# Cross attention on one core: inputs laid out by the host, the full-mask flag multiplied into Q, one key buffer, the loop written out

## The chip, the core and the metric

The kernel runs on one core of one Trainium2 chip. The core has TensorE (PE in the rows), VectorE (DVE), ScalarE (ACT), GpSimd (POOL) and SyncE (SP, which here only issues DMAs). Each works through its own instructions in order, and they meet at semaphores that the kernel sets and waits for by hand. The metric is the time of one execution on the device in microseconds. What the host does to the arrays before the launch isn't in it.

## The reference

```python
q = split_heads(x   @ W_Q.T)      # x: [4, 1024, 256], 16 heads of 16
k = split_heads(ctx @ W_K.T)      # ctx: [4, 77, 256]
v = split_heads(ctx @ W_V.T)
scores = q @ k.T / 4              # [4, 16, 1024, 77]
scores = where(mask == 1, -1e9, scores)
p = softmax(scores)
out = (p @ v).reshape(B, S, 256) @ W_O.T + x
out = (out - mean) * rsqrt(var + 1e-5) * gamma + beta     # over the 256
```

The mask is int32, [4, 1024, 77], and can mask all keys of a row. Such a row has equal scores, so its softmax is uniform.

## The kernel before, in words

The 4096 query rows are cut into 8 blocks of 512, two for each of the 4 batches. A block has 8 steps, one for each pair of heads, and its work is spread over three rounds of the loop, so that the engines work on several blocks at once.

Two blocks ahead (`n + 2`): x is scaled by a flag that is 0 for rows with all keys masked (`act_xs`, `pool_xs`), turned by TensorE (`pe_x_t`, steps 0 and 1, copied out by `act_x_t`), and projected to Q in two halves of 8 heads (`pe_q`, steps 2 and 3). Q is split into a high f16 part (`act_q_high`) and a low f16 part, the remainder (`dve_q_low`). SyncE writes both to a scratch tensor in DRAM (`store_q`) and reads them back by head (`load_q`) into `R`, which holds for each head the rows of a wide contraction: Q high, Q low, Q high again, the mask of the 77 keys (`load_mask`), and a row for the negated maximum. There are two buffers `R`, used in turn. The heads are loaded in the three groups of `GROUPS`: heads 0 to 5, 6 to 11, 12 to 15.

One block ahead (`n + 1`): the row maxima. `pe_max` computes scores with the queries on the partitions, in 12 units (3 groups by 4 tiles of 128 queries, 6 or 4 heads each, two banks in turn), `dve_max` reduces each to a maximum. `UNITS_AT` places two units in each of steps 0 to 5. `pe_nm` turns the maxima, `act_nm` copies them and ScalarE's queue issues the DMA that puts them in R's last row.

The block itself (`n`): `pe_scores` computes the transposed scores, keys on the partitions, less the maxima; ScalarE takes the exponential; `pe_pv` multiplies with the values, four heads side by side, after each 4 pairs; `dve_turn` turns the result and takes the reciprocal of the sum; `pool_norm` normalizes; `dve_ctx_e` turns back. The output projection of block `n - 1` (`pe_out`, f32, steps 6 and 7), the residual and the layer norm follow one and two rounds later.

The order on each queue is written out by hand in `body` of each engine. SyncE's matters here. In a round it stores half 0 of Q, then for each head group loads the mask, and Q (lines 316 to 325), and half 1's store stands between group 0's mask and group 0's Q:

```python
store_q(sp, n + 2, h, b + 1, 0)
for g in range(len(GROUPS)):
    sp.wait_ge(scores_done, PAIRS * n + GROUPS[g][1] // 2)
    load_mask(sp, n + 2, h, g)
    if g == 0:
        store_q(sp, n + 2, h, b + 1, 1)
```

The first and the last batch are written out; the two in the middle are one loop with a register. Because addresses in the loop depend on it, the keys and values of a batch are copied to fixed buffers (`kb_max`, `kb_scores`, `v_now`).

The setup turns the four weights, the context and the first blocks' x and masks on TensorE, projects K and V for all batches, and sends K through a DRAM scratch tensor like Q. Then it makes the whole of block 0's maxima (all 12 units of `pe_max` in a row).

Of the kernel before, what the change touches and what calls it, by code (L numbers as in the profile page):

```python
# [21 lines left out]
BLOCKS = BATCH * SEQ // BLOCK  # L45
TILES = BLOCK // P
HALVES = D // P
PAIRS = HEADS // 2
STEPS = PAIRS
QROWS = 3 * DK  # L50
MASK_ROW = QROWS
MAX_ROW = MASK_ROW + KEYS
KROWS = MAX_ROW + 1
BIG = 32768.0

GROUPS = [(0, 6), (6, 12), (12, 16)]
# [8 lines left out]
NM_AT = 5  # L65
XT_AT = (0, 1)
Q_AT = (2, 3)
OUT_AT = (6, 7)
STATS_AT = (0, 1, 2, 3)
VARIANCE_AT = 5  # L70
APPLY_AT = (6, 7)

CTX_AT = (1, 5)

LAST_VARIANCE_AT = 4
LAST_APPLY_AT = (5, 6)

POOL_TILES = TILES - 1

RLOADS = 3  # L80

GROUPS_OF = [[g for g, (lo, hi) in enumerate(GROUPS) if lo < (e + 1) * PAIRS and hi > e * PAIRS] for e in range(HALVES)]

MASK_PARTS = [(0, 1), (1, 2), (2, 4), (4, BLOCKS)]
MASK_LOADS = [(0, 1), (1, 4), (4, BLOCKS)]
MASK_TURNS = [(0, 1), (1, 2), (2, 4), (4, 6), (6, BLOCKS)]

WO_U, MASK_U = 5, 7
KSCALE = 1.0 / float(DK) ** 0.5

def cross_attention(nc, x, ctx_in, mask, w_q, w_k, w_v, w_o, gamma, beta, out):
    stack = ExitStack()
    with stack:
# [6 lines left out]
        def sem(name):  # L101
            return stack.enter_context(nc.semaphore(name))

        q_scratch = [nc.dram_tensor(f"q_scratch{i}", [HEADS, 2, DK, BLOCK], F16, kind="Internal").ap() for i in range(2)]
        k_scratch = nc.dram_tensor("k_scratch", [2, HEADS, DK, BATCH * KEYS], F16, kind="Internal").ap()

        x_all = sb("x_all", [P, BLOCKS * TILES, D])
        mask_all = sb("mask_all", [P, BLOCKS * TILES, KEYS], I32)  # L110
        w_t = [sb(f"w_t{i}", [P, HALVES, D]) for i in range(4)]
        ctx_sb = sb("ctx_sb", [KEYS, BATCH, D])
# [12 lines left out]
        minus_half = sb("minus_half", [P, TILES])
        all_masked = sb("all_masked", [P, BLOCKS * TILES])
        not_full = sb("not_full", [P, BLOCKS * TILES])
        not_full_big = sb("not_full_big", [P, BLOCKS * TILES])
        mask16 = sb("mask16", [P, BLOCKS * TILES, KEYS], F16)
        mask_t = sb("mask_t", [KEYS, BLOCKS, BLOCK], F16)  # L130
        xs = sb("xs", [P, TILES, D])
        x_t = sb("x_t", [P, HALVES, BLOCK])
        q16 = sb("q16", [P, HALVES, 2, BLOCK], F16)
        R = [sb(f"R{i}", [KROWS, HEADS, BLOCK], F16) for i in range(2)]
        neg_max = sb("neg_max", [P, TILES, HEADS], F16)
        neg_max_t = sb("neg_max_t", [HEADS, BLOCK], F16)
        probs = sb("probs", [P, PAIRS, 2, BLOCK])
        y = [sb(f"y{i}", [P, TILES, D]) for i in range(2)]

        spare = probs[:, 4:6, :, :].rearrange("p s i q -> p (s i q)").rearrange("p (i t d) -> p i t d", t=HALVES, d=D)  # L140
        w_in = [spare[:, i, :, :] for i in range(3)] + [y[1][:, 0:HALVES, :]]
        mask_eq = probs[:, 6:8, :, :].rearrange("p s i q -> p (s i q)").bitcast(F16)[:, 0:BLOCKS * TILES * KEYS].rearrange(
            "p (t k) -> p t k", k=KEYS)
        ctx_q = sb("ctx_q", [P, 2, BLOCK // 32, 32])
        rden = sb("rden", [P, 2, BLOCK // 32])
        ctx_n = sb("ctx_n", [P, HALVES, BLOCK // 32, 32])
        ctx_e = [sb(f"ctx_e{i}", [P, HALVES, BLOCK]) for i in range(2)]
        bn = sb("bn", [P, TILES, 6])
# [6 lines left out]

# [4 lines left out]
        work16 = work_ps[:, :].bitcast(F16)  # L160
        pv16 = pv_ps[:, :].bitcast(F16)
        max16 = [t[:, :].bitcast(F16) for t in max_ps]

        s_w = [sem(f"s_w{i}") for i in range(3)]
        s_ctx = sem("s_ctx")
        s_gb = sem("s_gb")
        s_x = [sem(f"s_x{i}") for i in range(BLOCKS)]
        s_mask = [sem(f"s_mask{i}") for i in range(len(MASK_LOADS))]
        s_ident = sem("s_ident")  # L170
        s_zero = sem("s_zero")
        w_t_done, w_t_ready = sem("w_t_done"), sem("w_t_ready")
        c_t_done, c_t_ready = sem("c_t_done"), sem("c_t_ready")
        k_done, k_high, k_low = sem("k_done"), sem("k_high"), sem("k_low")
        v_done, v_ready, v_ones = sem("v_done"), sem("v_ready"), sem("v_ones")
        s_k_out = sem("s_k_out")
        s_kb = sem("s_kb")
        tail_ready = sem("tail_ready")
        s_tail = [sem("s_tail_max"), sem("s_tail_scores")]
        kb_scores_ready, kb_max_ready, v_now_ready = sem("kb_scores_ready"), sem("kb_max_ready"), sem("v_now_ready")  # L180
        eq_ready, full_ready, not_full_ready, mask16_ready = sem("eq_ready"), sem("full_ready"), sem("not_full_ready"), sem("mask16_ready")
        xs_ready = sem("xs_ready")
        mask_t_done, mask_t_ready = sem("mask_t_done"), sem("mask_t_ready")
        x_t_done, x_t_ready = sem("x_t_done"), sem("x_t_ready")
        q_done, q_high, q_low = sem("q_done"), sem("q_high"), sem("q_low")
# [8 lines left out]
        bn_ready, mv_ready, ve_ready, rstd_ready, shift_ready = sem("bn_ready"), sem("mv_ready"), sem("ve_ready"), sem("rstd_ready"), sem("shift_ready")  # L194
        y_normed, y_gamma, y_beta = sem("y_normed"), sem("y_gamma"), sem("y_beta")
        y_dve = sem("y_dve")
        y_last = sem("y_last")
        s_y = [sem(f"s_y{i}") for i in range(2)]

        x_rows = x.rearrange("b (m p t) d -> p (b m) t d", p=P, t=TILES)
        mask_rows = mask.rearrange("b (m p t) k -> p (b m) t k", p=P, t=TILES)
# [13 lines left out]
        def store_q(sp, m, par, b, e):  # L216

            sp.wait_ge(q_low, HALVES * m + e + 1)
            if not isinstance(b, int) or b > 0:
                for g in GROUPS_OF[e]:  # L220
                    sp.wait_ge(s_R[par][g], 16 * RLOADS * b)
            for part in range(2):
                sp.dma_start(q_scratch[par][e * PAIRS:(e + 1) * PAIRS, part, :, :], q16[:, e, part, :]).then_inc(s_q_out[e], 16)  # L223

        def load_mask(sp, m, par, g):

            lo, hi = GROUPS[g]
# [786 lines left out]
```

## Time and profile before

| | |
|---|---|
| median of 3 runs | 223.49 us (222.67 to 225.48) |
| span of the profiled execution | 224.2 us |
| TensorE matmuls busy | 177.5 us (79%) |
| VectorE busy | 148.1 us (66%) |
| ScalarE busy | 113.7 us (51%) |
| GpSimd busy | 83.4 us (37%) |
| DMA | 33.35 MB, mean 149 GB/s |

The profile is one execution. Its record holds the span, 224.2 us, and that is its own time here; it lies between the slowest and the middle one of the three timed runs. Shares of the span mix the setup, the steady rounds and the tail, so a stage has to be read from the windows and from the instructions in order of time. In those, "[5.97 <-DMA R<-neg_max_t]" behind an instruction means that its engine stood idle for 5.97 us before it and what released it was a DMA that wrote R from neg_max_t.

### The profile page before, as it was taken

How to read it: one execution, taken by the hardware profiler on the slowest of the kernel's cores; microseconds unless marked ns; L12 is line 12 of the kernel's file. 1: busy time of each engine (PE TensorE's matmuls, PEld its weight loads, DVE VectorE, ACT ScalarE, POOL GpSimd, SP SyncE). 2: the span in 40 equal slices, each digit the busy share in tenths (PEclk: the TensorE clock that was granted, in tenths of full speed). 3: DMA queues.
4: the chain of work that ended last, by engine and by line, in shares of the span. 5: the costliest groups of instructions: out<-in, count | busy, mean ns of one | idle time of the engine just before them, and what ended most of it. 6: DMA issues, size and time to landing. Idle time of an engine off the chain costs nothing.

```text
span 224.2 us, 3953 instructions
## 1 busy us (share of the span) xinstructions
PE 177.5 (79%) x1264; PEld 98.9 (44%) x1264; DVE 148.1 (66%) x343; ACT 113.7 (51%) x161; POOL 83.4 (37%) x86
## 2 busy tenths in 40 slices
PE   2398536805988699999999999999999789899600
PEld 1364226503643363664555466445546335343500
DVE  4336054702457278589878859987885986667995
ACT  3044040611557274763697479369747635874020
POOL 1334900005401411111265149126414913865862
PEclk9999965995599699999999999999999969999995
DMA  6957959983897954771683475368448520020114
GB/s 185 315 190 214 114 127 185 242 158 102 145 382 194 186 128 127 173 166 33 200 189 140 129 201 135 135 192 167 154 136 191 136 96 3 0 95 3 80 37 164
DMA packets 28540, 33.35 MB, mean 149 GB/s; under 512 B 1949, under 2 KB 26193, under 8 KB 28525
## 3 DMA queue, kind: packets, MB, share of 16 engines
q1 hardware_dynamic: 28269, 33.03, 56.1%
q10 hardware_dynamic: 256, 0.13, 0.4%
q8 instruction: 8, 0.13, 0.3%
q14 instruction: 7, 0.06, 0.1%
HBM read 13.85 MB, written 8.70 MB: 101 GB/s over the span
## 4 chain that ended last, share of the span: by engine, by line
PE 45%; DVE 19%; DMA 14%; issue 7%; SPq 6%; ACT 4%; POOL 2%; DVEq 1%; ACTq 0%; POOLq 0%
PE work_ps L847 8%; PE work_ps L857 8%; PE pv_ps L827 8%; PE scores_ps L791 8%; DVE neg_max L601 7%; DMA x_all<-in_x 6%; PE max_ps L807 5%; PE work_ps L841 3%; DMA probs<-in_L_xattn_W_Q 3%; DMA k_scratch<-k 3%; DVE ctx_q L610 3%; DMA q_scratch<-q 3%; DVE bn L634 2%; ACT probs L555 1%; SPq L223 1%
## 5 line engine op out<-in xcount | busy, mean ns | idle before, releaser
L555 ACT ACTIVATE probs<-scores_ps 77x1024 f32<-77x1024 f32 x64 | 63.8, 1013 | 23.1 <-PE scores_ps L791 18.3
L601 DVE TENSOR_REDUCE neg_max<-max_ps 128x6 f16<-128x462 f32 (+1 forms) x96 | 51.3, 575 | 22.7 <-PE max_ps L807 22.3
L791 PE MATMUL scores_ps<-R,kb_scores 126*77 126x512 f16 x128 | 40.6, 402 | 9.7 <-DMA R<-neg_max_t 6.0
L368 POOL TENSOR_TENSOR ctx_n<-ctx_q,rden 128x256 f32<-128x256 f32 x32 | 20.2, 632 | 67.3 <-DVE rden L612 63.1
L807 PE MATMUL max_ps<-kb_max,R 125*128 125x77 f16 x512 | 32.7, 214 | 11.7 <-DMA R<-q_scratch 7.5
L807 PEld LDWEIGHTS max_ps<-kb_max,R 125*128 125x128 f16 x512 | 27.5, 107 | 27.5 <-issue 8.9
L827 PE MATMUL pv_ps<-probs,v_now 128*32 128x512 f32 x248 | 34.4, 628 | 0.0
L610 DVE STREAM_TRANSPOSE ctx_q<-pv_ps 128x512 f32<-128x512 f32 x31 | 21.9, 707 | 9.2 <-PE pv_ps L827 9.0
L857 PE MATMUL work_ps<-w_t,ctx_e 128*128 128x256 f32 x112 | 27.3, 386 | 0.4 <-DVE ctx_e L618 0.4
L847 PE MATMUL work_ps<-x_t,w_t 128*128 128x512 f32 x52 | 25.9, 620 | 0.5 <-DVE q L593 0.5
L791 PEld LDWEIGHTS scores_ps<-R,kb_scores 126*77 126x77 f16 x128 | 13.4, 122 | 26.0 <-issue 19.6
L857 PEld LDWEIGHTS work_ps<-w_t,ctx_e 128*128 128x128 f32 x112 | 20.4, 189 | 9.8 <-DVE y L625 5.9
L358 POOL TENSOR_TENSOR xs<-x_all,not_full 128x1024 f32<-128x1024 f32 x4 | 7.7, 1928 | 36.1 <-DMA x_all<-in_x 31.9
L495 ACT ACTIVATE y<-y,shift,rstd 128x256 f32<-128x256 f32 x27 | 14.6, 590 | 11.8 <-POOL shift L378 11.8
L470 ACT ACTIVATE q<-work_ps 128x512 f16<-128x512 f32 x13 | 7.8, 597 | 22.5 <-PE work_ps L847 22.5
L382 POOL TENSOR_TENSOR y<-y,gamma_sb 128x1024 f32<-128x1024 f32 (+1 forms) x7 | 16.0, 2286 | 5.9 <-ACT y L495 5.9
L625 DVE TENSOR_TENSOR y<-work_ps,x_all 128x512 f32<-128x512 f32 x14 | 9.7, 692 | 11.9 <-PE work_ps L857 11.8
L376 POOL TENSOR_TENSOR rstd<-var_eps,minus_half 128x4 f32<-128x4 f32 x8 | 8.5, 1059 | 23.1 <-DVE neg_mean L650 23.1
L388 POOL TENSOR_TENSOR y<-y,beta_sb 128x1024 f32<-128x1024 f32 (+1 forms) x7 | 16.2, 2315 | 0.4
L847 PEld LDWEIGHTS work_ps<-x_t,w_t 128*128 128x128 f32 x52 | 9.2, 195 | 11.7 <-issue 6.9
L593 DVE TENSOR_TENSOR q<-work_ps,q 128x512 f16<-128x512 f32 x13 | 8.9, 687 | 6.2 <-ACT q L470 6.2
L618 DVE STREAM_TRANSPOSE ctx_e<-ctx_n 128x512 f32<-128x512 f32 x16 | 11.2, 698 | 0.2 <-POOL ctx_n L368 0.2
(95 smaller groups left out, 177.4 us busy)
## 6 DMA issues: line engine op xcount, KB each, us to landing
R<-mask_t SPq DMA_DIRECT2D x16, 462.0 KB
x_all<-in_x SPq DMA_DIRECT2D x8, 512.0 KB, 7.7
q_scratch<-q SPq DMA_DIRECT2D x32, 128.0 KB
R<-q_scratch SPq DMA_DIRECT2D x16, 192.0 KB
out<-y SPq DMA_DIRECT2D x6, 512.0 KB, 2.6
R<-mask_t SPq DMA_DIRECT2D x8, 308.0 KB
R<-q_scratch SPq DMA_DIRECT2D x16, 96.0 KB
R<-q_scratch SPq DMA_DIRECT2D x8, 128.0 KB
```

Of the source, the lines that this page charges most:

```text
L368: nc.gpsimd.tensor_tensor(ctx_n[:, v, :, u * DK:(u + 1) * DK], ctx_q[:, t % 2, :, 0:DK], rden[:, t % 2, :].unsqueeze(2).to_broadcast([P, B ...
L382: nc.gpsimd.tensor_tensor(y[par][:, 0:tiles, :], y[par][:, 0:tiles, :], gamma_sb[:, :].unsqueeze(1).to_broadcast([P, tiles, D]), ALU.mult) ...
L388: nc.gpsimd.tensor_tensor(y[par][:, 0:tiles, :], y[par][:, 0:tiles, :], beta_sb[:, :].unsqueeze(1).to_broadcast([P, tiles, D]), ALU.add).t ...
L495: last = nc.scalar.activation(y[par][:, t, :], y[par][:, t, :], ACT.Identity, bias=shift[:, t:t + 1], scale=rstd[:, t:t + 1])
L555: nc.scalar.activation(probs[0:KEYS, s, :, :], scores_ps[s % 2][0:KEYS, :, :], ACT.Exp).then_inc(exp_done, 1)
L601: nc.vector.tensor_reduce(neg_max[:, t, lo:hi], max_ps[u % 2][:, 0:(hi - lo) * KEYS].rearrange("p (h k) -> p h k", k=KEYS), AX.X, ALU.max, ...
L610: nc.vector.transpose(ctx_q[:, t % 2, :, :], bank[:, :]).then_inc(pv_turned, 1)
L791: last = nc.tensor.matmul(scores_ps[s % 2][0:KEYS, i, :], kb_scores[:, 2 * s + i, :], R[par][:, 2 * s + i, :], start=True, stop=True)
L807: last = nc.tensor.matmul(max_ps[u % 2][:, i * KEYS:(i + 1) * KEYS], R[par][0:MAX_ROW, lo + i, t * P:(t + 1) * P], kb_max[0:MAX_ROW, lo + ...
L827: last = nc.tensor.matmul(bank[32 * j:32 * (j + 1), :], v_now[:, 8 * v + 2 * j + u, :], probs[:, 4 * v + j, u, :], start=True, stop=True)
L847: last = nc.tensor.matmul(bank[:, :], w_t[0][:, t, e * P:(e + 1) * P], x_t[:, t, :], start=(t == 0), stop=(t == HALVES - 1))
L857: last = nc.tensor.matmul(bank[:, i * D:(i + 1) * D], ctx_e[par][:, v, q0:q0 + P], w_t[3][:, v, :], start=(v == 0), stop=(v == HALVES - 1))
```

## The change

The host now hands over: x as before, x with the 256 features on the partitions (`x_cols`), the context and the four weights turned, and the mask with the keys on the partitions, one block a piece. The columns of W_Q and W_K are put in an order that makes each head group contiguous for a partition in the scratch tensors. The kernel has no transposes of inputs any more.

The flag for rows with all keys masked is made by a matmul with ones that counts the masked keys (`count`), and ScalarE's sign function (`nf`). It no longer scales x: it is multiplied into the projected Q on VectorE (`q_scale`), which writes an f32 tile, `q32`. ScalarE makes the high part from it, GpSimd the low part. x is loaded a second time, as rows, for the residual.

One buffer `kb` holds the keys of all batches with the mask and the ones rows. The loop is written out for all 8 blocks. Probabilities and values stand on 77 partitions, not padded to 128.

Positions also move: the halves of Q are projected at steps 1 and 5 instead of 2 and 3, the high part of half 1 is made at step 7, the units are at `UNITS_AT = [3, 2, 3, 2, 2, 0, 0, 0]`, the values' matmuls at steps 2, 4, 6 and the next 0, the output projection at steps 3 and 7. GpSimd computes variance and mean corrections (`moments`).

The core of the diff; the added parts of the kernel are from after the change:

```diff
-UNITS_AT = [2, 2, 2, 2, 2, 2, 0, 0]
-PV_AT = (0, 3, 5, 7)
-XT_AT = (0, 1)
-Q_AT = (2, 3)
-OUT_AT = (6, 7)
+UNITS_AT = [3, 2, 3, 2, 2, 0, 0, 0]
+X_RING = 3
+Y_RING = 4
...
@@ SyncE @@
+            def load_q(m, g):
+                lo, hi = GROUPS[g]
+                for e in range(HALVES):
+                    if hi > e * PER_HALF:
+                        sp.wait_ge(s_q_out[e], 32 * (m + 1))
+                if m >= 2:
+                    sp.wait_ge(scores_done, PAIRS * (m - 2) + hi // 2)
+                sp.dma_start(R[m % 2][Q_ROW:Q_ROW + 2 * DK, lo:hi, :],
+                             q_scratch[m % 2][:, :, lo:hi, :].rearrange("l d h q -> (l d) h q")).then_inc(s_R[m % 2][g], 16)
+                sp.dma_start(R[m % 2][Q_ROW + 2 * DK:MAX_ROW, lo:hi, :], q_scratch[m % 2][0, :, lo:hi, :]
+                             ).then_inc(s_R[m % 2][g], 16)
...
+            load_mask_i(0)
+            sp.dma_start(wk_t[:, :, :], w_k).then_inc(s_wk, 16)
+            load_xt(0)
+            load_mask_i(1)
+            load_xt(1)
+            for g in range(len(GROUPS)):
+                load_mask(0, g)
+            sp.wait_ge(k_low, HALVES)
+            for part in range(2):
+                for e in range(HALVES):
+                    sp.dma_start(k_scratch[part, :, e * PER_HALF:(e + 1) * PER_HALF, :], k16[:, part, e, :]).then_inc(s_k_out, 16)
+            store_q(0, 0)
+            sp.wait_ge(s_k_out, 64)
+            sp.wait_ge(tail_ones, 1)
+            for i, part in enumerate((0, 0, 1)):
+                sp.dma_start(kb[Q_ROW + i * DK:Q_ROW + (i + 1) * DK, :, :, :],
+                             k_scratch[part].rearrange("d h (b k) -> d h b k", b=BATCH)).then_inc(s_kb, 16)
+            store_q(0, 1)
+            for g in range(len(GROUPS)):
+                load_q(0, g)
+            load_mask_i(2)
+            for g in range(len(GROUPS)):
+                load_mask(1, g)
+            load_xt(2)
+            for e in range(HALVES):
+                store_q(1, e)
+            for g in range(len(GROUPS)):
+                load_q(1, g)
...
+            for n in range(N):
+                if n + 3 < N:
+                    load_mask_i(n + 3)
+                    load_xt(n + 3)
+                load_x(n)
+                if n + 2 < N:
+                    store_q(n + 2, 0)
+                    load_mask(n + 2, 0)
+                    load_mask(n + 2, 1)
+                    store_q(n + 2, 1)
+                    load_q(n + 2, 0)
+                    load_q(n + 2, 1)
+                    load_mask(n + 2, 2)
+                    load_q(n + 2, 2)
+                if n >= 2:
+                    store_y(n - 2)
...
@@ GpSimd @@
+            for n in range(N):
+                if n >= 1:
+                    norm(n - 1, 3)
+                if n >= 2:
+                    moments(n - 2)
+                if n + 2 < N:
+                    q_lo(n + 2, 0)
+                norm(n, 0)
+                if n >= 2:
+                    times_gamma(n - 2, 0)
+                norm(n, 1)
+                if n >= 2:
+                    times_gamma(n - 2, 1)
+                if n + 2 < N:
+                    q_lo(n + 2, 1)
...
@@ ScalarE @@
+            for n in range(N):
+                for s in range(STEPS):
+                    exp(n, s)
+                    if n + 2 < N:
+                        if s == 0:
+                            nf(n + 2, work_ps)
+                        if s == 2:
+                            q_hi(n + 2, 0)
+                        if s == 7:
+                            q_hi(n + 2, 1)
+                    if s == 5 and n + 1 < N:
+                        turn_max(n + 1)
+                    if s in (3, 4, 5, 6) and n >= 2:
+                        apply(n - 2, s - 3)
...
@@ VectorE @@
+            def q_scale(m, e, bank):
+                dve.wait_ge(q_done, HALVES * m + e + 1)
+                dve.wait_ge(nf_ready, m + 1)
+                if m > 0:
+                    dve.wait_ge(q_low, HALVES * (m - 1) + e + 1)
+                nc.vector.tensor_tensor(q32[:, e, :], bank, not_full[m % 2][:, :], ALU.mult).then_inc(q_scaled, 1)
...
+                for s in range(STEPS):
+                    if s == 2 and n + 2 < N:
+                        q_scale(n + 2, 0, work_ps[:, :])
+                    if s == 4 and n >= 1:
+                        residual(n - 1, 0)
+                    if n + 1 < N:
+                        for u in range(UNITS_AT[s]):
+                            reduce_max(n + 1, UNIT_START[s] + u)
+                    if s == 0:
+                        if n >= 2:
+                            residual(n - 2, 1)
+                        if n >= 1:
+                            turn(n - 1, 3)
...
+                    if s == 6:
+                        if n + 2 < N:
+                            q_scale(n + 2, 1, work_ps[:, :])
...
@@ TensorE @@
+            def max_unit(m, u):
+                (lo, hi), t = GROUPS[u // TILES], u % TILES
+                if t == 0:
+                    pe.wait_ge(s_R[m % 2][u // TILES], 16 * LOADS_R * (m // 2 + 1))
+                if UNITS * m + u >= 2:
+                    pe.wait_ge(max_reduced, UNITS * m + u - 1)
...
+            for n in range(N):
+                for s in range(STEPS):
+                    scores(n, s)
+                    if n + 1 < N:
+                        for u in range(UNITS_AT[s]):
+                            max_unit(n + 1, UNIT_START[s] + u)
+                        if s == 5:
+                            turn_max(n + 1)
+                    if s == 0 and n >= 1:
+                        values(n - 1, 3)
+                    if s in (2, 4, 6):
+                        values(n, s // 2 - 1)
+                    if n + 2 < N:
+                        if s == 0:
+                            if n >= 2:
+                                pe.wait_ge(out_ready, 2 * (n - 1))
+                            count(n + 2, work_ps)
+                        if s == 1:
+                            pe.wait_ge(nf_ready, n + 3)
+                            project_q(n + 2, 0, work_ps[:, :])
+                        if s == 5:
...
+                            project_q(n + 2, 1, work_ps[:, :])
```

## Rows read from the trace of the kernel before

**Rows 1.** Stage windows: length, busy us of each engine, granted TensorE clock, DMA share, GB/s.
```profile
core 0: us, PE busy (x) PEld busy (x) DVE busy (x) ACT busy (x) POOL busy (x), PEclk, DMA share, GB/s
...
51.00:55.00 4.00, 2.14 (x15) 1.17 (x16) 1.19 (x2) 1.02 (x1) 2.19 (x2) 0.50 0.26 75
...
74.00:76.00 2.00, 1.12 (x7) 0.64 (x8) 0.00 (x0) 0.04 (x1) 1.43 (x1) 0.58 0.87 186
76.00:78.00 2.00, 2.00 (x19) 0.72 (x16) 1.19 (x2) 0.98 (x1) 0.00 (x0) 0.57 0.99 177
...
134.40:153.70 19.30, 19.18 (x149) 10.52 (x148) 16.38 (x39) 13.57 (x22) 8.56 (x9) 1.00 0.59 157
```

**Rows 2.** TensorE in order of time, block 4: start us, us, instruction.
```profile
134.37 0.60 PE L791 MATMUL scores_ps<-R,kb_scores 126*77 126x512 f16 x2
134.80 0.61 PE L807 MATMUL max_ps<-kb_max,R 125*128 125x77 f16 x12
...
136.36 0.66 PE L841 MATMUL work_ps<-ident,xs 128*128 128x128 f32 x4
136.85 0.60 PE L791 MATMUL scores_ps<-R,kb_scores 126*77 126x512 f16 x2
...
151.91 1.99 PE L857 MATMUL work_ps<-w_t,ctx_e 128*128 128x256 f32 x8
153.74 0.60 PE L791 MATMUL scores_ps<-R,kb_scores 126*77 126x512 f16 x2
```

**Rows 3.** TensorE in order of time, setup, block 0 and start of block 6.
```profile
5.21 1.29 PE L877 MATMUL scores_ps<-ident,ctx_sb 77*128 77x77 f32 x8 [0.45 <-DMA ctx_sb<-in_ctx]
...
30.39 0.94 PE L807 MATMUL max_ps<-kb_max,R 125*128 125x77 f16 x12 [5.07 <-DMA R<-q_scratch]
...
35.40 0.96 PE L807 MATMUL max_ps<-kb_max,R 125*128 125x77 f16 x12 [2.47 <-DMA R<-q_scratch]
...
51.12 1.04 PE L791 MATMUL scores_ps<-R,kb_scores 126*77 126x512 f16 x2 [5.97 <-DMA R<-neg_max_t]
53.05 0.94 PE L807 MATMUL max_ps<-kb_max,R 125*128 125x77 f16 x12 [0.89 <-issue]
...
70.21 0.60 PE L791 MATMUL scores_ps<-R,kb_scores 126*77 126x512 f16 x2
...
74.88 1.04 PE L791 MATMUL scores_ps<-R,kb_scores 126*77 126x512 f16 x2 [3.08 <-issue]
...
173.67 0.61 PE L807 MATMUL max_ps<-kb_max,R 125*128 125x77 f16 x12
```

**Rows 4.** SyncE's DMA issues in order of time: start us, us of issuing.
```profile
31.66 0.44 SPq L236 DMA_DIRECT2D R<-q_scratch  x1
...
147.08 1.22 SPq L223 DMA_DIRECT2D q_scratch<-q  x2
148.43 0.39 SPq L234 DMA_DIRECT2D R<-q_scratch  x1
148.87 0.43 SPq L236 DMA_DIRECT2D R<-q_scratch  x1
```

**Rows 5.** Groups of instructions: shapes, count, busy us, mean ns, idle before.
```profile
L555 ACT ACTIVATE probs<-scores_ps 77x1024 f32<-77x1024 f32 x64 | 63.8, 1013 | 23.1 <-PE scores_ps L791 18.3 <-ACT neg_max_t L477 4.8
L601 DVE TENSOR_REDUCE neg_max<-max_ps 128x6 f16<-128x462 f32 x64 | 37.5, 627 | 18.7 <-PE max_ps L807 18.5
L382 POOL TENSOR_TENSOR y<-y,gamma_sb 128x1024 f32<-128x1024 f32 x6 | 14.2, 2367 | 4.3 <-ACT y L495 4.3
L470 ACT ACTIVATE q<-work_ps 128x512 f16<-128x512 f32 x13 | 7.8, 597 | 22.5 <-PE work_ps L847 22.5
L887 PE MATMUL max_ps<-ctx_t,w_t 128*128 128x308 f32 x8 | 3.2, 538 | 0.0
```

**Rows 6.** All transfers into and out of R, as far as someone waited for them.
```profile
DMA to landing us min/median/max: 2.1/4.4/8.8
```

**Rows 7.** The chain that ended last, setup: start us, us, what.
```profile
16.26 6.30 DMA k_scratch<-k
...
25.54 5.76 DMA q_scratch<-q
```

More of the change, by code:

```diff
@@ L181, in cross_attention @@
[L181 to L185, printed above, removed]
+        max16 = max_ps[0][:, :].bitcast(F16)
+        count_ps = [work_ps, pv_ps]
+        q_ps = [[scores_ps[m][:, e, :] for e in range(HALVES)] for m in range(2)]
@@ L216, in store_q @@
[L216 to L227, printed above, removed]
-            sp.dma_start(R[par][MASK_ROW:MAX_ROW, lo:hi, :],
-                         mask_t[:, bass.ds(m, 1), :].to_broadcast([KEYS, hi - lo, BLOCK])).then_inc(s_R[par][g], 16)
@@ L772, in _ @@
+            dve.wait_ge(mv_ready, TILES * N)
             for t in range(TILES):
[L773 to L776 removed]
+                nc.vector.scalar_tensor_tensor(out=rows[:, t, :], in0=rows[:, t, :], scalar=mean_var[:, t, 0:1],
+                                               in1=gamma_sb[:, :], op0=ALU.subtract, op1=ALU.mult).then_inc(last_scaled, 1)
+            dve.wait_ge(rstd_ready, N)
@@ new lines, in turn_max, with scores @@
+            def turn_max(m):
+                pe.wait_ge(max_reduced, UNITS * (m + 1))
+                for t in range(TILES):
+                    last = nc.tensor.transpose(max16[0:HEADS, t * P:(t + 1) * P], neg_max[:, t, :], ident16[:, :])
+                last.then_inc(nm_done, 1)
+            def scores(n, s):
+                if s == 0:
+                    pe.wait_ge(s_nm, 16 * (n + 1))
+                if PAIRS * n + s >= 2:
+                    pe.wait_ge(exp_done, PAIRS * n + s - 1)
+                for i in range(2):
+                    last = nc.tensor.matmul(scores_ps[s % 2][0:KEYS, i, :], kb[:, 2 * s + i, n // PER_BATCH, :],
+                                            R[n % 2][:, 2 * s + i, :], start=True, stop=True)
+                last.then_inc(scores_done, 1)
@@ new lines, in values, with project_out @@
+            def values(n, t):
+                pe.wait_ge(exp_done, PAIRS * n + 2 * (t + 1))
+                if QUADS * n + t >= 1:
+                    pe.wait_ge(pv_turned, QUADS * n + t)
+                for j in range(4):
+                    last = nc.tensor.matmul(pv_ps[32 * j:32 * (j + 1), :], v_all[:, n // PER_BATCH, 4 * t + j, :],
+                                            probs[:, 2 * t + j // 2, j % 2, :], start=True, stop=True)
+                last.then_inc(pv_done, 1)
+            def project_out(n, half):
+                if half == 0:
+                    pe.wait_ge(ctx_e_ready, HALVES * (n + 1))
+                for i in range(2):
+                    q0 = (2 * half + i) * P
+                    for v in range(HALVES):
+                        last = nc.tensor.matmul(work_ps[:, i * D:(i + 1) * D], ctx_e[n % 2][:, v, q0:q0 + P], wo_t[:, v, :],
+                                                start=(v == 0), stop=(v == HALVES - 1))
+                last.then_inc(out_done, 1)
```

1083 lines of the change are left out of this document (387 added, 696 removed).

## The prediction

> **What bounds the kernel now.** I read the stage windows first, then TensorE's instructions in order of time, then the costliest groups and SyncE's queue. The stage windows give one block of the steady part, 134.4 to 153.7 us: TensorE is busy 19.18 of 19.30 us, VectorE 16.38, ScalarE 13.57, GpSimd 8.56, the DMA engines 0.59 of the time, at the full clock of 2.4 GHz [rows 1]. Block 4's first scores start at 134.37 and block 5's at 153.74 [rows 2]: 19.37 us a block, all TensorE. Around it lie a setup that waits for transfers (the first max matmuls at 30.39, the first scores at 51.12 after 5.97 us of waiting for the negated maxima's DMA, the second block's max at 53.05), a slow block 0 that ends at 74.88, and from 173.67 on the last two blocks with the tail, 50.5 us [rows 3].
>
> What matters for the change is that in the kernel before TensorE never waits for Q in the steady part: both halves of block n+2's Q are projected at steps 2 and 3, stored by 148.30 and re-read for the first head group at 148.43 [rows 4], 5 us ahead of the block that uses them.
>
> **The change, part by part.**
>
> *TensorE, steady.* Two transpose steps a block go. One takes 136.36 to 136.85, 0.49 us [rows 2]; two, 0.97. The count matmul comes: one f16 matmul of 512 columns, half of a scores step (134.37 to 134.80, 0.43), 0.22. New TensorE work: 19.37 - 0.97 + 0.22 = 18.62 us a block. Alone that would be worth 0.75 x 6 = 4.5 us.
>
> *ScalarE, VectorE, GpSimd.* ScalarE loses the copies of x and the scaled x, gains a sign of 512 columns: it stays near 12 us, hidden. VectorE swaps q_low for q_scale of the same shape, loses the variance steps and the copies of keys and values, gains a comparison and a mask product on 77x512: at most what it had, 16.4, hidden as a sum. GpSimd gains two q_lo a block. No row shows that form; the gamma product is 2367 ns for 1024 columns [rows 5], so 512 cost 1.18, and below that I bound it by the 0.6 of ScalarE's copy of the same tile [rows 5]; I take 1.05, near the same-engine row because the engine decides. As a sum GpSimd stays near 11 of 18.6 us.
>
> *Third max units.* Steps 0 and 2 now hold three units instead of two over two buffers, so the third waits for a reduce (627 ns, [rows 5]). Laying out step 0 (reduces, residual, turn, then the wait for `nf`) and step 2 (q_scale ahead of three reduces) gives 1.6 us of TensorE waiting a block; bounds 0 (VectorE ahead) and 3.
>
> *The queue order, the step that decides.* Q of half 1 is projected at step 5 and `q_hi(n+2, 1)` stands on ScalarE behind `exp(n, 7)`, the last of the block. `q_lo` follows on GpSimd. On SyncE `store_q(n+2, 1)` stands ahead of `load_q(n+2, 0)`, so even the first head group, which needs only half 0, is queued behind it. And TensorE's in-order queue meets that group, `max_unit(n+2, 0)`, as the second thing in block n+1. From the end of `scores(n, 7)`:
> - exp(n, 7), 1.01 [rows 5]
> - q_hi, 0.60 [rows 5]
> - q_lo, 1.05
> - two store issues, 1.22 [rows 4]
> - two load issues, 0.39 + 0.43 [rows 4]
> - landing. In the setup the last issue of group 1's pair ended at 32.10 [rows 4] and its max matmuls began at 35.40, waiting for it [rows 3]: 3.3. Bounds are 2.1, the shortest landing of a transfer into R [rows 6], and 5.8, a q store in the full queue of the setup [rows 7]. I take 3.3, the only row of this same transfer that somebody waited for
> - six handoffs, 0.35.
>
> Sum 8.35 us. The cover in that time is one output half (151.91 to 153.74, 1.83) and a scores pair (0.43) [rows 2]: 2.27. So TensorE stands idle about 6.1 us at the start of blocks 1 to 6. Behind it wait the max units, then the count, `nf`, the exponentials: everything.
>
> *The clock.* After the 3.08 us wait before 74.88 the windows 74 to 76 and 76 to 78 were granted 0.58 and 0.57, so both hold much of the lower level, 1.2 GHz [rows 1, 3]; about 3 us at half clock loses 1.5. In 51 to 55, after 5.97 us, it was 0.50 [rows 1]. Part of the slow stretch falls where TensorE waits for reduces anyway; I take 1.0 a block, bounds 0.5 and 4. The Trainium skill ("TensorE: Matmul & The Clock Gate", section HAM oscillation) speaks against this change: a kernel that waits for a DMA in each iteration starts each one throttled. The trace of before shows the fall after single waits, and none in its steady part.
>
> Period: 8.35 + (18.62 - 2.27) + 1.6 + 1.0 = 27.3 us, where it was 19.4.
>
> *The landing, by the skill.* "DMA: Bandwidth & Descriptors", section on the anatomy of one DMA, gives about 2.0 us fixed per transfer on its software path; by that estimate each landing would be 1.3 shorter than my 3.3 and the total some 8 us less. The rows of before do not show this transfer alone.
>
> *Setup.* Gone: waiting for W_Q's transpose, context and x transposes, kb copies on ScalarE. Added: K stores as four issues, half-by-half. The K projection can start when W_K and the context are in (the context was at 5.21 [rows 3]); it is 3.2 us [rows 5] and ends near 8.4; k_low near 9.4, against 16.26 as the start of the K store before [rows 7]. Four stores at 0.6 are issued by 11.7 and landed near 15 to 18 (one of the whole took 6.3 [rows 7]), the kb loads are issued near 17, the store of half 1 and the first q loads near 19, landing in the 5.8 of a full queue [rows 7]: first max near 24 to 25, where it was 30.39 [rows 3]. Twelve units at the reduces' pace, 7 us, the transposes and the negated maxima's DMA follow, with 1.2 MB of block 1's masks and 0.5 MB of x ahead in the queue: first scores and block 1's max matmuls near 41 against 53.05. Gain 12; bounds 5 (each landing 2 us worse) and 25 (each at the 2.1 of [rows 6]).
>
> *Block 0.* From its first max matmul at 53.05 to the end of its last scores (70.21 + 0.60 [rows 3]) it took 17.8. Off come two transposes at half clock, 1.8, a wait for xs, 0.85, mask transposes, 0.9; on come the count and the third units, 2.0: 16.3. Its last scores end at 57.3, R(2) is there at 57.3 + 8.35 = 65.7.
>
> *The sum.* Five periods of 27.3 to R(7): 202.2. From there before took 50.5 us [rows 3]; block 6 starts slow (+1.0) and VectorE has less in it (-1.0). 252.7; I round to **252 us**, against 224.2 in this profile and 223.5 as the median, which differ less than a term here.
>
> Extra traffic (x twice, 0.5 MB, and the mask, 0.15 MB a block) costs nothing: the engines are 0.59 busy of 19.3 and the period is longer; uncovered it would be about 3 us a block. Loop unrolling: nothing; before shows no gap at block borders.
>
> **Rivals.**
> A. *Short landings, faster.* The deciding quantity is how long a transfer takes from issue to semaphore. At 2.1 [rows 6] in every hop, with no third-unit waits and 0.5 of clock, the chain is 7.1, the period 23.95; setup reaches block 1's max near 28, block 0's last scores near 42.5, R(2) at 49.6, R(7) at 169.6, end 220; with q_lo at 0.6 besides, 217. For it: larger contiguous packets in the q loads. Against: the two of the busy setup took 5.8 and 6.3 [rows 7]. Some eleven hops stand on the path (five in setup, six chains), so it crosses the old time at a landing of 2.5 everywhere. Chance 5%.
> B. *The clock stays low.* After waits of 6 us TensorE was at 0.50 in 51 to 55 [rows 1] and had to be busy long before it rose. If half of each period runs at 1.2 GHz, 3 us more a block, six times: about 270. For: the wait is 6.1, like that one. Against: 74 to 78 recovered in 3 us. Chance 15%.
> C. *Middle: landings near 2.6 and VectorE half ahead.* Chain 7.65, waits 0.8, clock 0.8: period 25.6, setup 15 gained: 240. Chance 22%.
> D. *The order costs nothing*, because the stores end before the block does and TensorE stays the bound at 18.6: 224.2 - 12 - 4.5 = 208. It would need ScalarE to reach q_hi some 6 us earlier than `exp(n, 7)`, which its in-order queue excludes. 3%.
> Forecast itself 55%.
>
> **Numbers.** 252 with C and B inside and the low bounds of landing and third units: 233 to 270. A measurement of this kernel tells about 2% (219 to 228) from no change. Faster 0.06 (A's lower part, D), same 0.06 (A's upper part, C's tail), slower 0.88.
>
> **What would show it.** In the changed profile: TensorE idle 5 to 7 us once a block, before a max group, released by the DMA into R, six times; ScalarE's q copy right behind the block's last exponential; SyncE's first q load of a block after its last q store; low clock at each block's start; first scores near 40; blocks of 27 us. I am wrong if the max groups start without a wait for R, or if setup ends before 32.

## The result and the profile after

The changed kernel takes 269.0 us (268.29 and 269.65), the kernel before 223.34 in the same session: ratio 1.201, 95% interval 1.191 to 1.211. Two further executions of the changed kernel took 273.14 and 274.42 us at a lower granted clock, and such slow executions are left out of every time given here for a changed kernel. It is slower, as forecast, by 46 us. The forecast was 252 with a range of 233 to 270, so the measured time lies inside the range, 1 us below its upper end. The profiled execution is the one of 269.65 us. Its span, from the first instruction to the last, is 267.8 us, and the sums below are made against that.

TensorE in order of time in the changed kernel (start us, us, instruction; in brackets the idle time ahead and its releaser):

```profile
26.94 0.58 PE L603 MATMUL max_ps<-kb,R 125*128 125x77 f16 x12 [4.19 <-DMA R<-q_scratch]
32.27 1.12 PE L603 MATMUL max_ps<-kb,R 125*128 125x77 f16 x12 [4.75 <-DVE neg_max L455]
...
44.49 1.04 PE L620 MATMUL scores_ps<-R,kb 126*77 126x512 f16 x2 [5.07 <-DMA R<-neg_max_t]
45.33 0.98 PE L603 MATMUL max_ps<-kb,R 125*128 125x77 f16 x12
...
60.88 0.62 PE L620 MATMUL scores_ps<-R,kb 126*77 126x512 f16 x2
...
70.35 0.96 PE L603 MATMUL max_ps<-kb,R 125*128 125x77 f16 x12 [7.59 <-DMA R<-q_scratch]
...
99.93 0.96 PE L603 MATMUL max_ps<-kb,R 125*128 125x77 f16 x12 [6.52 <-DMA R<-q_scratch]
...
119.06 0.62 PE L620 MATMUL scores_ps<-R,kb 126*77 126x512 f16 x2
119.53 1.89 PE L639 MATMUL work_ps<-wo_t,ctx_e 128*128 128x256 f32 x8
121.85 0.62 PE L620 MATMUL scores_ps<-R,kb 126*77 126x512 f16 x2 [0.44 <-DMA R<-neg_max_t]
128.22 0.96 PE L603 MATMUL max_ps<-kb,R 125*128 125x77 f16 x12 [5.74 <-DMA R<-q_scratch]
...
133.93 3.36 PE L590 MATMUL work_ps<-x_t,wq_t 128*128 128x512 f32 x4
137.13 0.60 PE L620 MATMUL scores_ps<-R,kb 126*77 126x512 f16 x2
...
216.21 0.96 PE L603 MATMUL max_ps<-kb,R 125*128 125x77 f16 x12 [6.08 <-DMA R<-q_scratch]
```

The steady part is where the time went. Where the block before went from max unit to max unit in 19.4 us without a gap [rows 2], this one waits for R at the head of each of blocks 1 to 6, and its periods are 29.6, 28.3, 29.4, 28.5 and 30.2 us: 145.9 us from 70.35 to 216.21. Against that, block 1's max units start at 45.33, not 53.05 [rows 3]. The six waits for Q sum to 37.3 us (7.59, 6.52, 5.74, 5.65, 5.69 and 6.08). The last stretch is 51.6 us, before 50.5.

The chain ahead of 128.22, on three queues. ScalarE, then GpSimd, then SyncE:

```profile
119.73 1.02 ACT L375 ACTIVATE probs<-scores_ps 77x1024 f32<-77x1024 f32 x1
120.65 0.61 ACT L359 ACTIVATE q<-q 128x512 f16<-128x512 f32 x1
```

```profile
121.34 1.15 POOL L263 TENSOR_TENSOR q<-q 128x512 f16<-128x512 f32 x1 [0.30 <-ACT q L359]
```

```profile
122.52 1.20 SPq L172 DMA_DIRECT2D q_scratch<-q  x2
123.81 0.55 SPq L190 DMA_DIRECT2D R<-q_scratch  x1
124.42 0.42 SPq L192 DMA_DIRECT2D R<-q_scratch  x1
```

Read down: the last exponential of the block, the high part of half 1 right behind it, the low part, the stores, and only then the loads of a group that needs half 0 alone. Issued at 124.84, they have landed at 128.22.

The stage windows (length, busy us of PE, PEld, DVE, ACT, POOL, granted clock, DMA share, GB/s):

```profile
core 0: us, PE busy (x) PEld busy (x) DVE busy (x) ACT busy (x) POOL busy (x), PEclk, DMA share, GB/s
...
128.20:137.20 9.00, 8.63 (x46) 4.07 (x47) 5.53 (x10) 1.71 (x2) 0.62 (x1) 0.52 0.76 247
137.20:151.00 13.80, 13.18 (x95) 6.83 (x93) 10.76 (x26) 9.68 (x13) 6.70 (x10) 1.00 0.30 90
```

After the wait TensorE is busy 8.63 of 9.00 us and still at 1.2 GHz nearly all that time (0.52). The Q projection of half 0 takes 3.36 us; in e3 below, at full clock, it takes 1.98. The kernel before was at 1.00 throughout its steady block [rows 1].

### The profile page after: what moved, and what is told of

The parts are those of the page before. It is cut to its first block, busy times and chain, and to the rows that moved or that the text cites. A ratio compares the mean times of both kernels' runs of the same rounds, so it can differ in the third digit from the quotient of the medians.

```text
span 267.8 us, 3437 instructions
## 1 busy us (share of the span) xinstructions
PE 181.5 (68%) x1152; PEld 91.1 (34%) x1152; DVE 141.9 (53%) x302; ACT 99.8 (37%) x129; POOL 91.9 (34%) x120
## 2 busy tenths in 40 slices
DMA packets 22904, 37.18 MB, mean 139 GB/s; under 512 B 2384, under 2 KB 17232, under 8 KB 22840
## 4 chain that ended last, share of the span: by engine, by line
PE 23%; issue 19%; POOL 18%; DMA 14%; DVE 12%; SPq 7%; ACT 4%; DVEq 1%; ACTq 0%; POOLq 0%
DMA R<-q_scratch 7%; DVE neg_max L455 7%; PE pv_ps L629 6%; POOL y L290 6%; PE max_ps L603 6%; PE work_ps L590 5%; POOL q L263 4%; PE scores_ps L620 4%; POOL ctx_n L270 3%; POOL rstd L281 3%; DMA mask_i<-in_mask_cols 3%; SPq L172 2%; DMA R<-neg_max_t 2%; DMA q_scratch<-q 2%; ACT probs L375 2%
## 5 line engine op out<-in xcount | busy, mean ns | idle before, releaser
L603 PE MATMUL max_ps<-kb,R 125*128 125x77 f16 x512 | 36.3, 230 | 53.6 <-DMA R<-q_scratch 41.5
L603 PEld LDWEIGHTS max_ps<-kb,R 125*128 125x128 f16 x512 | 29.9, 117 | 69.8 <-DMA R<-q_scratch 40.1
L620 PE MATMUL scores_ps<-R,kb 126*77 126x512 f16 x128 | 42.7, 419 | 8.1 <-DMA R<-neg_max_t 7.7
L629 PE MATMUL pv_ps<-probs,v_all 77*32 77x512 f32 x256 | 39.3, 690 | 2.3 <-ACT probs L375 1.9
L263 POOL TENSOR_TENSOR q<-q 128x512 f16<-128x512 f32 x16 | 18.8, 1174 | 57.5 <-ACT q L359 57.5
L590 PE MATMUL work_ps<-x_t,wq_t 128*128 128x512 f32 x48 | 28.4, 722 | 0.0
L620 PEld LDWEIGHTS scores_ps<-R,kb 126*77 126x77 f16 x128 | 13.0, 125 | 43.9 <-issue 29.4
L639 PE MATMUL work_ps<-wo_t,ctx_e 128*128 128x256 f32 x112 | 27.0, 384 | 0.5 <-DVE ctx_e L471 0.5
L290 POOL TENSOR_TENSOR y<-y,gamma_sb 128x512 f32<-128x512 f32 x14 | 17.8, 1272 | 20.0 <-ACT y L380 20.0
L380 ACT ACTIVATE y<-y,shift,rstd 128x256 f32<-128x256 f32 x28 | 16.3, 593 | 16.4 <-POOL shift L283 13.5
L639 PEld LDWEIGHTS work_ps<-wo_t,ctx_e 128*128 128x128 f32 x112 | 20.7, 190 | 4.1 <-issue 1.0
L296 POOL TENSOR_TENSOR y<-y,beta_sb 128x512 f32<-128x512 f32 x14 | 17.8, 1288 | 0.0
```

The lines of the kernel that those rows point to most:

```text
L263: nc.gpsimd.tensor_tensor(q16[:, e, 1, :], q32[:, e, :], q16[:, e, 0, :], ALU.subtract).then_inc(q_low, 1)
L290: nc.gpsimd.tensor_tensor(rows, rows, gamma_sb[:, :].unsqueeze(1).to_broadcast([P, 2, D]), ALU.mult).then_inc(y_gamma, 1)
L296: nc.gpsimd.tensor_tensor(rows, rows, beta_sb[:, :].unsqueeze(1).to_broadcast([P, 2, D]), ALU.add).then_inc(y_beta, 1)
L590: last = nc.tensor.matmul(bank, wq_t[:, t, e * P:(e + 1) * P], x_t[m % X_RING][:, t, :], start=(t == 0), stop=(t == HALVES - 1))
L603: last = nc.tensor.matmul(max_ps[u % 2][:, (h - lo) * KEYS:(h - lo + 1) * KEYS], R[m % 2][0:MAX_ROW, h, t * P:(t + 1) * P], kb[0:MAX_ROW, ...
L620: last = nc.tensor.matmul(scores_ps[s % 2][0:KEYS, i, :], kb[:, 2 * s + i, n // PER_BATCH, :], R[n % 2][:, 2 * s + i, :], start=True, stop ...
```

## The experiments

The theory was that an order is what costs: `q_hi` behind the last exponential, and `load_q` of group 0 behind `store_q` of half 1. The rivals were volume (x goes over the DMA engines twice), VectorE with the third max units, and the clock alone. The runs were made in three sessions (e1 to e4, e5 to e8, e9 and e10), each with executions of the kernel before beside them. The ratio is to those, so it is the better measure between sessions.

### e1, one line on SyncE

```diff
                     load_mask(n + 2, 1)
-                    store_q(n + 2, 1)
                     load_q(n + 2, 0)
+                    store_q(n + 2, 1)
                     load_q(n + 2, 1)
```

> The changed kernel with one line moved on SyncE: the Q loads of head group 0 (which need half 0 alone) stand ahead of the store of half 1. The theory (TensorE waits for a chain exp, q_hi, q_lo, stores, load, landing) says: max units 0 to 3 no longer wait; the wait moves to unit 4, whose load is issued 6.0 to 6.8 us after the block's last scores and lands 3.4 us later, at 10.2, where unit 4 now runs 14.0 us after them. 3.8 us less for each of six blocks, and somewhat less time at the low clock: 243 to 250 us. Rival, transfers limited by volume (x is loaded twice): the same bytes move, so 268 to 274. Rival, VectorE's order sets the period: unchanged too.

Measured: 245.4 us, ratio to before 1.111 (1.101 to 1.121). One line is worth 23.5 us by the times and 20 by the ratios, and not a byte is moved less, so volume isn't the cause of that part. TensorE in e1:

```profile
115.60 0.62 PE L620 MATMUL scores_ps<-R,kb 126*77 126x512 f16 x2 [1.14 <-DMA R<-neg_max_t]
117.59 0.60 PE L603 MATMUL max_ps<-kb,R 125*128 125x77 f16 x12 [1.37 <-DMA R<-q_scratch]
```

At the head of this block 1.14 us are left of waiting for the negated maxima and 1.37 for Q. My expectation had the wait for Q at unit 4. In blocks 1 and 2 it was there (1.14 and 2.91 us, at 70.33 and 96.10); from block 3 on unit 0 waited as well, for a reason that the next run shows better. And although the wait was that short, the window from 117.5 to 126.1 was granted 0.60.

### e2, half 1 of Q early

```diff
 # TensorE: project_q(n + 2, 1) at s == 3, project_out(n - 1, 0) at s == 5
 # VectorE: q_scale(n + 2, 1) at s == 4, residual(n - 1, 0) and stats(n - 1, 0) at s == 6
 # ScalarE
-                        if s == 7:
+                        if s == 4:
                             q_hi(n + 2, 1)
 # GpSimd
                 norm(n, 0)
+                if n + 2 < N:
+                    q_lo(n + 2, 1)
                 if n >= 2:
                     times_gamma(n - 2, 0)
...
                     times_gamma(n - 2, 1)
-                if n + 2 < N:
-                    q_lo(n + 2, 1)
```

> The changed kernel with half 1 of Q projected at step 3 instead of 5, its scaling at step 4, its high part at step 4 instead of 7, its low part two places earlier on GpSimd; output half 0 moves to step 5, its residual to step 6. SyncE's order is untouched. The theory: half 1 is stored before the block ends, the wait for R vanishes, TensorE is the bound again at 18.6 to 20 us a block where it was 29.2; five periods and the first wait give 50 to 60 us: 211 to 220 us. Rival, the third max units, VectorE or the second copy of x are worth most of the loss: the period stays above 23 us and the time above 235.

Measured: 242.2 us, 1.086 (1.079 to 1.094). A gain of 27 us, where 50 to 60 were expected. GpSimd in e2:

```profile
99.93 0.20 POOL L283 TENSOR_TENSOR shift<-rstd,neg_mean 128x4 f32<-128x4 f32 x1
100.08 1.16 POOL L263 TENSOR_TENSOR q<-q 128x512 f16<-128x512 f32 x1
...
102.27 1.16 POOL L263 TENSOR_TENSOR q<-q 128x512 f16<-128x512 f32 x1 [0.45 <-ACT q L359]
```

SyncE in e2:

```profile
101.27 1.19 SPq L172 DMA_DIRECT2D q_scratch<-q  x2
102.55 1.89 SPq L180 DMA_DIRECT2D R<-mask_t  x2
104.55 3.13 SPq L172 DMA_DIRECT2D q_scratch<-q  x2
107.78 0.54 SPq L190 DMA_DIRECT2D R<-q_scratch  x1
```

The low part of half 0 stands behind the layer norm's moments (the shift at 99.93 is their last step), so both halves come out at nearly the same time. Two masks follow, 462 KB each, and behind them SyncE needs 3.13 us to issue two stores that took 1.20 in the changed kernel. The loads start at 107.8, 3.2 us later than the low part of half 1 would allow (103.4 plus 1.2 for the stores). TensorE waited 2.35 us at 111.74. The window from 111.7 to 120.3 was granted 0.60, so about 7 us of it were at 1.2 GHz, and the next one, to 134.8, 1.00.

### e3, the clock alone

```diff
+                        if s == 0 and n >= 1:
+                            for _ in range(6):
+                                nc.tensor.matmul(max_ps[1][:, :], wq_t[:, 0, 0:P], wo_t[:, :, :].rearrange("p t d -> p (t d)"),
+                                                 start=True, stop=True)
                         for u in range(UNITS_AT[s]):
                             max_unit(n + 1, UNIT_START[s] + u)
```

> The changed kernel with six added f32 matmuls of 512 columns (weights on weights, into the free second max bank, result unused) on TensorE just ahead of each block's first max unit from block 1 on; they fill the wait for R without changing what is waited for. 
Measured: 254.9 us, 1.140 (1.130 to 1.151). 14 us less for 5 us more of useless work a block. TensorE in e3:

```profile
119.34 5.32 PE L683 MATMUL max_ps<-wo_t,wq_t 128*128 128x512 f32 x12
125.05 0.60 PE L603 MATMUL max_ps<-kb,R 125*128 125x77 f16 x12 [0.40 <-DMA R<-q_scratch]
...
129.05 1.98 PE L590 MATMUL work_ps<-x_t,wq_t 128*128 128x512 f32 x4
130.87 0.60 PE L620 MATMUL scores_ps<-R,kb 126*77 126x512 f16 x2
```

```profile
core 0: us, PE busy (x) PEld busy (x) DVE busy (x) ACT busy (x) POOL busy (x), PEclk, DMA share, GB/s
97.50:99.80 2.30, 1.73 (x26) 0.89 (x26) 1.82 (x4) 0.00 (x0) 0.00 (x0) 1.00 0.87 190
99.80:103.20 3.40, 3.20 (x20) 1.77 (x17) 2.33 (x5) 1.71 (x2) 0.62 (x1) 0.50 1.04 273
...
110.00:150.00 40.00, 37.48 (x215) 17.99 (x214) 21.91 (x51) 20.41 (x27) 20.43 (x24) 1.00 0.53 156
```

From 110 to 150 us the clock is 1.00 throughout. There the stretch from the first max unit to the scores of step 2 takes 5.8 us (125.05 to 130.87). In the changed kernel it took 8.8, 7.7, 8.9, 7.9 and 9.0 us in five blocks, 8.5 on average. So the low clock costs 2.65 us in each of those on average. In the last of the six blocks, which has less work, the stretch is 5.3 us, and 3.3 in e3. Together that is 15 us. The filling didn't win all of it. It covers 5.3 us of each wait, and where more was left (2.36, 1.04 and 0.67 us, in the blocks that start at 70.21, 97.55 and 151.37) the clock fell for 3.4 us, as at 99.8 above, and the stretch took 6.9 to 7.4 us. In the other three, with 0.39 to 0.54 us left, it stayed at 1.00. The stretches are 11 us shorter in sum, the profiled spans differ by 12 and the times by 14. The 7.7 to 8.9 us in my expectation are the length of this stretch, and not the time at the low clock.

The Trainium skill ("TensorE: Matmul & The Clock Gate", HAM oscillation) describes a kernel that waits for a DMA in each iteration and starts each one throttled. The trace of the changed kernel agrees: behind the wait of 5.74 us, 128.2 to 137.2 was granted 0.52.

### e4, half 1's high part one step earlier

```diff
 # ScalarE
-                        if s == 7:
+                        if s == 6:
                             q_hi(n + 2, 1)
 # GpSimd
                 norm(n, 1)
-                if n >= 2:
-                    times_gamma(n - 2, 1)
                 if n + 2 < N:
                     q_lo(n + 2, 1)
+                if n >= 2:
+                    times_gamma(n - 2, 1)
```

> The changed kernel with the high part of half 1 made one step earlier on ScalarE (behind exponential 6, ahead of the layer norm's apply) and its low part on GpSimd ahead of the gamma product of the second half. Only the order changes. The theory: the copy starts near 119.2 instead of 120.65 and GpSimd's part is done 1.4 us earlier, so each of the six waits is 1.4 us shorter: 260 to 264 us. If the landing or the issue order were the cause and not this chain: no change, 268 to 274.

Measured: 259.8 us, 1.161 (1.151 to 1.171): 9 less. That is 1.5 a block where the chain was to be shortened by 1.4, and in the trace each wait is 1.6 to 2.1 us shorter. So the copy and the low part are links of the chain.

### e8, the setup's comparison behind the reduces

```diff
-            eq(2)
             for u in range(UNITS):
                 reduce_max(0, u)
+            eq(2)
```

> The changed kernel with VectorE's comparison of block 2's mask behind the twelve reduces of block 0, in place of ahead of them; in the changed kernel the reduces waited 4.4 us for it (the mask's DMA stands behind block 0's Q loads on SyncE). Block 0's maxima are then done 4.4 us earlier. If they set the start, 4 us less: 267. But block 1's Q loads are issued at 39.8 to 42.5 whatever VectorE does and block 1's max matmuls need them: then 0 to 1.5 us, 270 to 271.

Measured: 271.5 us, 1.209 (1.193 to 1.224), against 269.0 and 1.201 (1.191 to 1.211): no gain, and no difference clear of the noise. TensorE in e8:

```profile
34.74 0.59 PE L611 MATMUL max_ps<-ident,neg_max 128*16 128x128 f16 x4 [0.57 <-DVE neg_max L455]
40.78 1.04 PE L620 MATMUL scores_ps<-R,kb 126*77 126x512 f16 x2 [5.45 <-DMA R<-neg_max_t]
44.37 0.96 PE L603 MATMUL max_ps<-kb,R 125*128 125x77 f16 x12 [2.54 <-DMA R<-q_scratch]
```

Block 0's maxima are 4.1 us earlier (34.74, was 38.82), but block 1's max units start at 44.37, only 1.0 earlier: they now wait for block 1's Q, the late transfer behind the one that was taken away.

### e7, e1 and e2 together

The diff is e1's and e2's together.

> e1 and e2 together, nothing else. In e2 TensorE still waited 2.1 to 2.4 us, since the Q loads of group 0 stood behind two masks and both stores (issued at 107.8 with the low part ready at 103.4), and 8.6 us of low clock followed. With the loads ahead of the second store the wait is 0 to 1 us and the clock stays up: period 25.9 becomes 20.5 to 22, time 217 to 225. If GpSimd's late low part of half 0 (behind the moments) is the next bound, 225 to 235.

Measured: 234.4 us, 1.047 (1.034 to 1.060). Another 8 us on e2, not 20. It lands in the window given for the case in which GpSimd's late half 0 is the next bound. With Q of half 1 early, the order on SyncE is thus still worth 8 us here, while half 0 is late. And against e1, which has the better order and the late producer, early Q is worth 11.

### e5, all orders

```diff
 # e1 and e2 and e8, and:
 # GpSimd
-                if n >= 2:
-                    moments(n - 2)
                 if n + 2 < N:
                     q_lo(n + 2, 0)
+                if n >= 2:
+                    moments(n - 2)
 # SyncE
                     load_mask(n + 2, 0)
-                    load_mask(n + 2, 1)
                     load_q(n + 2, 0)
+                    load_mask(n + 2, 1)
                     store_q(n + 2, 1)
```

> All order repairs on the changed kernel: half 1 of Q at steps 3 and 4 (as in e2), Q loads of group 0 ahead of the store of half 1 (as in e1) and ahead of group 1's mask, half 0's low part ahead of the layer norm's moments on GpSimd, the comparison of block 2's mask behind block 0's reduces. Theory: no wait for R is left, TensorE at full clock, 19 to 20.5 us a block: 208 to 217 us, below the kernel before. Rival: the third units and VectorE keep the period at 22 or more: 225 or more.

Measured: 222.4 us, 0.990 (0.977 to 1.003). 12 us less than e7; level with the kernel before. It meets neither my 208 to 217 nor the rival's 225 or more. The three moves between e7 and e5 were not taken apart, except that e8's was worth nothing by itself.

### e6 and e9, the third units and the residual

```diff
 # e6
-UNITS_AT = [3, 2, 3, 2, 2, 0, 0, 0]
+UNITS_AT = [2, 2, 2, 2, 2, 2, 0, 0]
 # e9: e6, and on VectorE
+                    if s == 0 and n >= 2:
+                        residual(n - 2, 1)
                     if n + 1 < N:
                         for u in range(UNITS_AT[s]):
                             reduce_max(n + 1, UNIT_START[s] + u)
                     if s == 0:
-                        if n >= 2:
-                            residual(n - 2, 1)
```

> e5 with two max units in each of steps 0 to 5, as in the kernel before, in place of 3, 2, 3, 2, 2. The third units waited 0.35 and 0.52 us for a reduce, twice a block, when TensorE was fast. If these 0.9 us are worth their face, seven blocks give 4 to 6 us less than e5. If they only shift the wait to the transposed maxima of step 5 (two more units stand ahead of them), no difference or up to 3 us more.

> e6 with one more move: on VectorE the residual of the second half stands ahead of step 0's two reduces. In e6 the count matmul waited 0.67 us a block for that residual, which stood behind both reduces. TensorE is otherwise full there, so if this wait is on the path it gives 0.6 us in each of five blocks, 213 to 214.5 us; if the reduces, now 0.7 us later, hold the next max units instead, there is no difference from 216.6.

Measured: e6 216.6 us, 0.971 (0.960 to 0.982); e9 214.4 us, 0.965 (0.958 to 0.972). The third units cost 6 us by the times and 4 by the ratios. The intervals of e5 and e6 overlap a little, but every execution of e6 (216.5 to 218.9) is below every one of e5 (from 220.6). e9's move is worth 2 by the times; the two ratios' intervals overlap, so its size isn't settled, but the trace shows the wait gone. TensorE in e9:

```profile
124.37 0.61 PE L619 MATMUL scores_ps<-R,kb 126*77 126x512 f16 x2
...
126.34 0.39 PE L584 MATMUL work_ps<-eq,ones 77*128 77x512 f16 x1
...
137.48 0.39 PE L610 MATMUL max_ps<-ident,neg_max 128*16 128x128 f16 x4 [0.82 <-DVE neg_max L455]
...
143.34 0.60 PE L619 MATMUL scores_ps<-R,kb 126*77 126x512 f16 x2
```

The count has no wait ahead of it (0.67 us in e6), and this block takes 18.97 us, under the 19.4 of [rows 2]; the shortest steady block of e6 took 19.8. With its queues and units in order the changed kernel is 3.5% faster than the kernel before.

### e10, SyncE's order put back into e9

```diff
                     load_mask(n + 2, 0)
-                    load_q(n + 2, 0)
                     load_mask(n + 2, 1)
                     store_q(n + 2, 1)
+                    load_q(n + 2, 0)
```

> e9 with SyncE's order of the changed kernel put back (both masks and both stores of Q ahead of the Q loads of group 0), everything else repaired. It prices the queue order alone once Q itself is early. In e6 the second store was issued until 101.8 us and TensorE came to the max units at 106.0: the loads would be issued until 102.8 and land 3.4 us later, at 106.2, so the wait is 0 to 1 us a block and the time 0 to 6 us above e9. If the order is what cost in itself, as much as in e1 (24 us), then 235 or more.

Measured: 216.0 us, 0.969 (0.962 to 0.976), 1 to 2 us above e9, with a ratio inside e9's interval. Its trace still has a wait of 2.42 us for Q at block 1 and of 0.35 to 0.75 us at three later blocks. The same order on SyncE that cost more than 20 us in the changed kernel costs hardly anything that can be measured once both halves of Q are made early. So it isn't the order in itself; it is the order together with a late producer.

## Why the prediction came out as it did

**The bound and the mechanism: right.** It said that TensorE would wait for R's first group once a block, at blocks 1 to 6, through `exp(n, 7)`, `q_hi`, `q_lo`, the stores and the loads. The trace shows that chain, and e1, e2 and e4 shorten it at three different links with 23, 27 and 9 us.

**The chain's length: right.** Predicted 8.35 us from the last scores' end to R. Measured from 119.68 to 128.22: 8.54. Exponential 1.02 (1.01 said), low part 1.15 (1.05), two stores 1.20 (1.22), two loads 1.03 (0.82), landing 3.38 (3.3). The landing was taken from the one row of before in which somebody waited for that transfer, and it held although the kernel's packets are larger on average now (22904 for 37.18 MB, before 28540 for 33.35 MB). The prediction's other estimate for a landing, 2.0 us, would have been 1.4 short.

**The clock: the term that was mis-sized.** The forecast of 252 is 17 us short of the time, and this term is the largest part of that. It was 1.0 us a block, bounds 0.5 to 4. Measured 2.65 (e3). I priced it by the wait of 3.08 us in [rows 1, 3] that was followed by 3 us of low clock, and took off a share for overlap with the reduces. Read in windows of 0.5 us, the clock rose again only 5.9 to 8.7 us after these waits had ended. After the 5.97 us wait of [rows 3] it was 9.5 us. The wait I forecast, 6.1 us, was like that second one. Rival B said so with a chance of 15%. Its 3 us came on top of the 1.0, so it stood at 4.0, and 2.65 lies about midway between the two. In the sum the term alone is short by 1.65 x 5 = 8 us. That B's total of 270 comes within 1 us of the time is luck in part, since the setup and the tail, in which B changed nothing, add 5.4 us.

**The setup: too optimistic by 4.3 us.** Block 1's max units were forecast at 41 and started at 45.33; the gain was 7.7 and not 12. First max at 26.94 (24 to 25 said). The comparison that waited for a mask, which I had not seen, delayed the reduces by 4.4 us, but e8 shows that behind it Q of block 1 lands at about the same time: it was issued at 39.8, behind 1.2 MB of masks and 0.5 MB of x that I had counted in.

**The rest: right.** Block 0 from first max unit to the end of its last scores: 16.2 us, forecast 16.3. The tail 51.6, forecast 50.5. Together: 4.3 (setup) - 0.1 + 0.5 (first chain) + 9.4 (five periods) + 1.1 (tail) = 15.2, and 252.7 + 15.2 = 267.9, against a span of 267.8. The 1.2 us from there to the time of 269.0 are what timing adds to a span (269.65 for this execution of 267.8), less the spread between executions. Of the 9.4 us, 8 are the clock's.

**Third units: of the right order.** 1.6 us a block in the sum. e6 takes two in place of three and gains 4 to 6 us in all. In e3, at full clock, the gaps in front of the third units are 0.52 and 0.53 us and the count waits 0.34, together 1.4.

**What was costed at nothing.** The second copy of x: e9 moves the same bytes, at 18.97 us a block and a DMA share of 0.73 (124.4 to 143.3 us), so it is covered there as well. GpSimd's order was costed at nothing for half 0. In the changed kernel that was true, and in e2 it was not.

**Rivals.** A (short landings) fell: the landings were 3.4. D (the order costs nothing) fell with the six waits. C (240) fell. The gains that I counted for the change are real in part, as e9 shows: without the waits and the third units it is 3.5%, 8 us, faster than the kernel before, where D had 208.

## What to carry to other kernels

Where a result crosses several in-order queues, write down the chain from the last thing ahead of it on each queue to the first thing that waits for it, and compare it with the work that TensorE has in between; here 8.5 us stood against 2.3. A consumer's load that stands behind a late producer on another queue costs far more than either alone. The order was worth more than 20 us with Q late (e1), 8 with half 1 early and half 0 late (e7 against e2) and 1 to 2 with both halves early (e10). The late producer with the order right still cost 11 (e1 against e7). A wait of TensorE that comes once a loop is to be priced with the low clock behind it: here 2.65 us on top of each 6, and a wait of 2.35 us in e2 still brought about 7 us of low clock. After a repair look for what stood right behind the thing repaired (e8, e2).

## What the runs showed of the hardware

- TensorE, busy 8.63 of 9.00 us at the head of a block, was granted 0.52 for that window. It came back to 2.4 GHz 5.9 to 8.7 us after the waits of 5.7 to 7.6 us had ended, and about 3 us after the wait of 3.08 us in the kernel before. Filling the wait with useless matmuls kept it at 1.00 in three of six blocks, shortened the low stretch to 3.4 us in the others, and gave back 12 to 14 us.
- Issuing two stores of 128 KB took SyncE 1.20 us, and 3.13 us right behind two mask transfers of 462 KB (e2). In e1 and e7 two loads of Q issued right behind the masks took 3.0 and 2.9 us, against 1.0 in the changed kernel. That the queue was full is my guess; whether it is the bytes or the number of packets was not tested.
- The first comparison of 77x512 took 2.06 us, while GpSimd was filling a buffer; later ones took 0.38 to 0.55. The cause was not tested.

The first comparison and its like, VectorE in the changed kernel:

```profile
4.08 2.06 DVE L432 TENSOR_SCALAR eq<-mask_i 77x512 f16<-77x512 int32 x1 [4.08 <-DMA mask_i<-in_mask_cols]
...
118.98 0.38 DVE L432 TENSOR_SCALAR eq<-mask_i 77x512 f16<-77x512 int32 x1
```
